# The final norm of an adaLN block moved into the block of the expert tiles

## The reference

```python
out = sum over the token's two experts of weight * (gelu(x @ w_up[e].T) @ w_down[e].T)
mu = mean(out); var = mean(square(out - mu))
out = (out - mu) * rsqrt(var + 1e-5)
ffn = out + x                      # x: the normalised, shifted input h
result = x_before + gb * ffn       # gb: one row of 128 per batch
```

## Time and profile before

| | |
|---|---|
| median of 3 runs | 1081.94 us (1081.14 to 1083.57) |
| the profiled execution | 1080.8 us, its span 1078.9 us |
| PE busy | 927.0 us, 86% of the span |
| VectorE, ScalarE, GpSimd busy | 847.5 (79%), 730.2 (68%), 557.8 us (52%) |
| tile block ends, closing block begins | 1042.3 us |
| closing block | 36.6 us to the span's end |

### The profile page before, as it was taken

One profiled execution on the slowest core, in us unless ns is written; L12 is line 12 of the kernel. 1 busy time (PEld: TensorE's weight loads), 2 busy tenths in 40 slices (PEclk: granted clock), 3 DMA queues, 4 the chain that ended last, 5 costly groups with the idle time before them and its releaser, 6 DMA issues. The chain is left out here.

```text
span 1078.9 us, 20269 instructions
## 1 busy us (share of the span) xinstructions
PE 927.0 (86%) x6154; PEld 666.3 (62%) x6154; DVE 847.5 (79%) x1731; ACT 730.2 (68%) x1927; POOL 557.8 (52%) x634
## 2 busy tenths in 40 slices
PE   4599999999999999999999999999996179999800
PEld 2366666666666667667666667666664167888600
DVE  5478888788878888888888888788876569988627
ACT  2278777778777777877777777777774256667504
POOL 1245446444665557465556646564673606766610
PEclk9999999999999999999999999999998579999955
DMA  7222322232222222222322232223122756676334
GB/s 241 53 50 50 74 50 50 50 73 61 50 64 72 60 64 69 60 53 73 79 50 50 64 85 57 56 74 77 45 60 97 237 195 244 244 238 236 126 104 130
DMA packets 67227, 104.27 MB, mean 97 GB/s; under 512 B 11115, under 2 KB 49912, under 8 KB 63536
## 3 DMA queue, kind: packets, MB, share of 16 engines
q1 hardware_dynamic: 59056, 90.53, 29.2%
q0 software_dynamic: 4992, 8.94, 2.8%
q10 hardware_dynamic: 3072, 3.51, 0.9%
HBM read 21.09 MB, written 15.50 MB: 34 GB/s over the span
## 5 line engine op out<-in xcount | busy, mean ns | idle before, releaser
L1173 POOL TENSOR_TENSOR four<-four 128x512 f32<-128x512 f32 x128 | 161.2, 1281 | 334.5 <-DVE ot L1119 213.8
L996 ACT ACTIVATE prob<-ps,nmax 128x512 f32<-128x512 f32 (+3 forms) x512 | 264.5, 529 | 76.1 <-DVE nmax L1096 76.1
L1096 DVE TENSOR_REDUCE nmax<-ps 128x2 f32<-128x1024 f32 (+3 forms) x256 | 211.0, 824 | 8.8
L915 PE MATMUL ps<-ident,prob 128*128 128x128 f32 x1280 | 191.4, 279 | 12.2 <-ACT probt L1017 6.9
L915 PEld LDWEIGHTS ps<-ident,prob 128*128 128x128 f32 x1280 | 142.2, 141 | 62.5 <-ACT prob L996 36.7
L1177 POOL TENSOR_TENSOR qk_lo<-four,qk_hi 128x512 fp32r<-128x512 f32 x128 | 162.3, 1291 | 0.0
L937 PE MATMUL ps<-probt,val 128*64 128x512 f32 (+3 forms) x1024 | 153.6, 442 | 0.2 <-ACT probt L1017 0.2
L1089 DVE TENSOR_TENSOR ps<-ps,tri 128x256 f32<-128x256 f32 x256 | 109.3, 427 | 53.5 <-PE ps L894 52.7
L1024 ACT CAST qk_hi<-four 128x512 fp32r<-128x512 f32 x128 | 79.5, 621 | 96.7 <-POOL four L1173 96.7
L1017 ACT COPY probt<-ps 128x512 f32<-128x512 f32 (+2 forms) x256 | 124.7, 520 | 19.6 <-PE ps L915 19.6
L1585 POOL DMA_INDIRECT results<-y,to_i x92 | 96.6, 1050 | 73.0 <-DVE y L1429 50.7
(11 more groups left out here) (222 smaller groups left out, 2163.4 us busy)
## 6 DMA issues: line engine op xcount, KB each, us to landing
four<-four SPq DMA_DIRECT2D x256, 128.0 KB
wt<-wall SPq DMA_DIRECT2D x23, 1024.0 KB, 4.8
xg<-slots SPq DMA_DIRECT2D x23, 288.0 KB, 3.8
hb<-h_hi SPq DMA_DIRECT2D x64, 64.0 KB, 2.1
hb<-h_lo SPq DMA_DIRECT2D x64, 64.0 KB, 2.0
y<-results SPq DMA_DIRECT2D x8, 512.0 KB, 7.3
x_all<-in_x SPq DMA_DIRECT2D x4, 512.0 KB, 10.6
h_hi<-rows SPq DMA_DIRECT2D x8, 256.0 KB, 2.7
```

The lines of the kernel that those rows point to most:

```text
L915: mm = e.transpose(ps[:, PT + at % 2, at_block * P:(at_block + 1) * P], prob[:, unit, kk * P:(kk + 1) * P], ident[:])
L996: e.activation(prob[:, unit, 0:w], ps[:, bank_s(idx) + j, 0:w], ACT.Exp, bias=nmax[:, q.par, idx, j:j + 1], accum_out=den[:, q.par, 2 * i ...
L1096: e.tensor_reduce(nmax[:, q.par, idx, :], ps[:, bank:bank + 2, 0:w], AX.X, ALU.max, negate=True).then_inc(v_max, 1)
L1173: e.tensor_tensor(qk[:, cols], tt[:, cols], ur[:, cols], op=ALU.add).then_inc(g_qk, 1)
```

## The change

The closing block is gone; its work stands behind the tile loop in the tile block, on the same engines, so one block end with its barrier falls away. SyncE waits for the landed scatters and for the weight copies and then issues the eight loads. The loaded rows `y2` and the products `z` (now one for each batch) lie in the SBUF of `wall`. ScalarE writes the normalised batch b into PSUM bank (b + 4) mod 8, and VectorE multiplies out of that bank. The factors of the second half come after the first product in place of after four products and adds. GpSimd does the adds of batches 0 to 3, VectorE those of 4 to 7; SyncE stores in order of batches, on two semaphores. The functions `end_sums`, `end_begin` and `end_factors` hold the former instructions of L1644 to L1661 unchanged.

```diff
+            plain = wall[:].rearrange("p x k i -> p (x k i)").bitcast(F32)
+            y2 = plain[:, 0:NT * 2 * E].rearrange("p (n k f) -> p n k f", k=2, f=E)
+            z = plain[:, NT * 2 * E:NT * 2 * E + B * S].rearrange("p (a t f) -> p a t f", a=B, f=E)
+            minus = sb(ph, "minus", [P, NT])
...
+            def norm_of(b):
+                return ps[:, (b + 4) % B, :].rearrange("p (t f) -> p t f", f=E)
...
+            def load_results(e):
+                for p in range(3):
+                    e.wait_ge(d_wt[p], 16 * ((NTL + 2 - p) // 3))
+                for p in range(4):
+                    e.wait_ge(d_ys[p], 16 * TB * ((NTL + 3 - p) // 4))
+                yv = ys.rearrange("(n p k) f -> p n (k f)", p=P, k=2)
+                for b in range(B):
+                    n = slice(b * TB, (b + 1) * TB)
+                    e.dma_start(y2[:, n].rearrange("p n k f -> p n (k f)"), yv[:, n, :]).then_inc(d_y2[b], 16)
...
+            def end_norm(e, g):
+                n = half_rows(g)
+                e.wait_ge(v_var, g + 1)
+                e.activation(tmp[:, 3, n], tmp[:, 1, n], ACT.Sqrt).then_inc(a_root, 1)
+                for b in range(g * PER, (g + 1) * PER):
+                    e.wait_ge(v_fac, g + 1)
+                    e.wait_ge(v_y, NTL)
+                    for t in range(TB):
+                        m = b * TB + t
+                        ins = e.activation(norm_of(b)[:, t, :], y2[:, m, 0, :], ACT.Identity,
+                                           bias=minus[:, m:m + 1], scale=rstd[:, m:m + 1])
+                    ins.then_inc(a_z, 1)
+            def end_gate(e, b):
+                e.wait_ge(a_z, b + 1)
+                e.tensor_tensor(z[:, b], norm_of(b), over(b), op=ALU.mult).then_inc(v_z, 1)
+            def end_result(e, b):
+                m = slice(b * TB, (b + 1) * TB)
+                e.wait_ge(v_z, b + 1)
+                e.wait_ge(v_g, 2 * B)
+                e.tensor_tensor(x_all[:, m, :], x_all[:, m, :], z[:, b], op=ALU.add).then_inc(v_out[b // PER], 1)
@@ tile block, SyncE, after the tile loop
+                    load_results(e)
+                    for b in range(B):
+                        n = slice(b * TB, (b + 1) * TB)
+                        e.wait_ge(v_out[b // PER], b % PER + 1)
+                        e.dma_start(ov[:, n, :], x_all[:, n, :]).then_inc(d_out, 16)
+                    e.wait_ge(d_out, 16 * B)
@@ ScalarE, after the tile loop
+                    for g in range(HALVES):
+                        end_norm(e, g)
@@ VectorE, after the tile loop
+                    for b in range(PER):
+                        end_sums(e, b)
+                    end_begin(e, tick, 0)
+                    end_factors(e, tick, 0)
+                    for b in range(PER, B):
+                        end_sums(e, b)
+                    end_begin(e, tick, 1)
+                    end_gate(e, 0)
+                    end_factors(e, tick, 1)
+                    for b in range(1, PER):
+                        end_gate(e, b)
+                    for b in range(PER, B):
+                        end_gate(e, b)
+                        end_result(e, b)
@@ GpSimd, after the tile loop
-                    for p in range(4):
-                        e.wait_ge(d_ys[p], 16 * TB * ((NTL + 3 - p) // 4))
-        with ExitStack() as ph:
-            y2 = sb(ph, "y2", [P, NT, 2, E])
...
+                    for b in range(PER):
+                        end_result(e, b)
```

More of the change, by code:

```diff
@@ L1266, in adaln_kernel @@
             tiles = sb(ph, "tiles", [P, 4, NTL])
+            plain = wall[:].rearrange("p x k i -> p (x k i)").bitcast(F32)
+            y2 = plain[:, 0:NT * 2 * E].rearrange("p (n k f) -> p n k f", k=2, f=E)
+            z = plain[:, NT * 2 * E:NT * 2 * E + B * S].rearrange("p (a t f) -> p a t f", a=B, f=E)
+            minus = sb(ph, "minus", [P, NT])
+            HALVES = 2
+            NH2 = NT // HALVES
+            PER = B // HALVES
+            d_y2 = [sem(f"e_y2{b}") for b in range(B)]
@@ new lines, in adaln_kernel, with half_rows @@
+            v_sum, v_st, v_dve, v_var, a_root, v_fac, a_z, v_z, v_out0, v_out1, d_out = (
+                sem("e_" + n) for n in ("sum", "st", "dve", "var", "root", "fac", "z", "vz", "out0", "out1", "dout"))
+            v_out = (v_out0, v_out1)
+            def norm_of(b):
+                return ps[:, (b + 4) % B, :].rearrange("p (t f) -> p t f", f=E)
+            def half_rows(g):
+                return slice(g * NH2, (g + 1) * NH2)
+            def load_results(e):
[7 more added lines that the diff above has]
+                    e.dma_start(y2[:, n].rearrange("p n k f -> p n (k f)"), yv[:, n, :]).then_inc(d_y2[b], 16)
@@ new lines, in end_sums, with end_begin @@
+            def end_sums(e, b):
+                m = slice(b * TB, (b + 1) * TB)
+                e.wait_ge(d_y2[b], 16)
+                e.tensor_tensor(y2[:, m, 0, :], y2[:, m, 0, :], y2[:, m, 1, :], op=ALU.add).then_inc(v_sum, 1)
+                e.wait_ge(v_sum, b + 1)
+                for t in range(TB):
+                    e.bn_stats(stats[:, b * TB + t, :], y2[:, b * TB + t, 0, :]).then_inc(v_st, 1)
+            def end_begin(e, tick, g):
+                n = half_rows(g)
+                e.wait_ge(v_st, NH2 * (g + 1))
+                factors_begin(v_dve, tick, e, lambda k: stats[:, n, k], mean[:, n],
+                              [tmp[:, i, n] for i in range(3)]).then_inc(v_var, 1)
@@ new lines, in end_factors @@
+            def end_factors(e, tick, g):
+                n = half_rows(g)
+                e.wait_ge(a_root, g + 1)
+                factors_end(v_dve, tick, e, rstd[:, n], tmp[:, 3, n], [tmp[:, i, n] for i in range(3)]).then_inc(v_dve, 1)
+                e.wait_ge(v_dve, tick.after(1))
+                e.scalar_tensor_tensor(out=minus[:, n], in0=mean[:, n], scalar=-1.0, in1=rstd[:, n],
+                                       op0=ALU.mult, op1=ALU.mult).then_inc(v_fac, 1)
+            def end_norm(e, g):
+                n = half_rows(g)
+                e.wait_ge(v_var, g + 1)
[3 more added lines that the diff above has]
+                    e.wait_ge(v_y, NTL)
+                    for t in range(TB):
+                        m = b * TB + t
+                        ins = e.activation(norm_of(b)[:, t, :], y2[:, m, 0, :], ACT.Identity,
+                                           bias=minus[:, m:m + 1], scale=rstd[:, m:m + 1])
+                    ins.then_inc(a_z, 1)
@@ L1483, in _ @@
                             copy_weights(e, j, col)
+                    load_results(e)
+                    ov = out.rearrange("(n p) f -> p n f", p=P)
+                    for b in range(B):
[3 more added lines that the diff above has]
+                    e.wait_ge(d_out, 16 * B)
                 @block.tensor
@@ L1575, in _ @@
                             dve_y(e, q // IC)
+                    tick = Count()
+                    for b in range(PER):
[12 more added lines that the diff above has]
+                        end_result(e, b)
                 @block.gpsimd
```

## The result

The changed kernel took 1071.67 us (median of 4 runs, 1069.55 to 1073.9), the kernel before in the same comparison 1082.76 us (4 runs, 1081.14 to 1084.12). The two medians lie 11.1 us apart. The ratio on record is 0.9914 with a 95% interval of 0.9895 to 0.9934, which is 7.1 to 11.4 us of the kernel before.

A forecast was written before the change was run, and what follows sets the result against it. After the last tile, VectorE's 23.1 us wait, with GpSimd's 8.882 us drain in it, was taken as the bound. Span 1078.9 to 1069.9 saves 9.0 us: 1071.8 from the profiled run, 1072.9 from the median; prediction 1072.4, range 1067.5 to 1075.5.

The forecast's parts named there:

- Boundary: Between tile loop and closing work: SyncE takes over the scatter waits, so the loads go out 9.3 us earlier.
- Rival C: At the old block end: the drain waited for the scatters' data, so no change, 1081.1 us; chance 0.03.
- D: In the tile loop: ScalarE table loads of 1.28 us placed at each of 23 tiles, 1101 us; chance 0.02.
- Price of the drain: GpSimd's drain, now at the program's end: 0.082 us per scatter since the last drain, 8.9 us for 108.
- A: At the closing drain: cost is time since the last scatter, so already settled, 1068.7 us; chance 0.14.
- E: At the closing drain: VectorE holds off its reads and stretches it by up to 3.3 us, 1075.1 us; chance 0.06.
- Hold-off: GpSimd's adds beside VectorE: whoever starts first holds off the other's two-SBUF-input instruction; second-half factors 1.15 us late.
- Rival B: GpSimd's adds beside VectorE: no contention, drain and barrier end at 1068.1, time 1070.0 us; chance 0.16.
- The end: Program end: GpSimd's drain from 1060.8 costs 8.9 us, the barrier 0.25, giving span 1069.9.
- the other branch: VectorE's adds and the stores at the end: VectorE done at 1064.1, plus 2.7 us, ending at 1066.8.

The follow-up runs named there:

- E4: The kernel before, its closing block and order untouched, without the GpSimd drain at the end of the tiles' block: 1086.63 us, ratio 0.9928.
- E1: The changed kernel with one more GpSimd drain, right behind its last scatter and ahead of its four adds: 1083.38 us, ratio 0.9881.
- E7: The changed kernel with a further GpSimd drain after tile 11 of 23: 1081.16 us in one run.
- E2: The changed kernel with the adds of batches 0 to 3 on VectorE instead of GpSimd: 1083.08 us, ratio 0.9883.
- E6: The changed kernel with an early GpSimd drain and GpSimd's first add held back until the second half's factors are ready: 1077.51 us, ratio 0.9888.
- E3: The changed kernel with only the block end removed: old order, all adds on VectorE, normalised rows in SBUF: 1088.99 us, ratio 0.9941.
- E10: The changed kernel with an early GpSimd drain and all four first-half products ahead of the second half's factors: 1073.26 us in one run.

## Why the prediction was right

Point by point, with the predicted distances from the first load's issue (1033.05 there, 1031.17 measured):

- *Boundary.* Predicted 9.3 us, measured 9.6 in the stretch from the last scatter to the first load (11.87 against 2.27). SyncE sees the last scatter land 2.3 us behind its start; GpSimd's drain and the barrier are what stood between. E4 shows the drain to be the cause and the barrier worth 0.7 us. Rival C is out. The first load landed in 4.0 us (3.9 predicted), and from there no table load delays anything: the changed kernel has five in all, as before, and Sqrt's stands at 1019.86, ahead of the loads (D is out). One small misreading: VectorE is not without a gap from 1046.25 on, it stands 0.28 us for the first root, in both kernels.
- *Price of the drain.* Predicted 8.9 us behind GpSimd's fourth add, measured 8.9. E1, E4 and E7 show that it goes by the number of scatters and not by time or place. A is out, and so is E, by which VectorE's work would have stretched it: VectorE worked for the first 3.2 us of the drain, and it took 8.9 all the same.
- *Hold-off.* Predicted for the squaring: a delay of 1.15 us; measured 1.01 (1.18 instead of 0.17). GpSimd's fourth add was predicted 27.75 us behind the first load, measured 27.35; VectorE's last add 31.05 and 30.55. Both came earlier, in part since the adds were stretched less than forecast: VectorE's by 0.6 and 0.35 us, GpSimd's last three by 0.3 together (4.17 against three of 1.28). E2 and E6 take the overlap away and the 1.2 us with it. Rival B is out.
- *The end.* Predicted span end 36.85 us behind the first load, measured 36.5. The predicted time, 1072.4, is 0.7 above the measured median, and some of this nearness is luck: in the profiled executions the forecast was 1071.8 against 1069.55, of which 0.6 us is an error of the stretch (9.0 forecast, 9.6 measured) and 1.6 lie ahead of the last scatter, where the forecast saw no change and no run explains one.

One step was wrong though its number was not. The prediction let the other branch end 2.7 us behind VectorE's last add, 33.75 us behind the first load, and gave batch 4's store 3 us of slack. In fact five stores were bunched behind GpSimd's fourth add, and SyncE saw the last of them land 6.0 us behind it, 33.3 us behind the first load; with the 0.4 us of the barrier that is 33.7. So nothing showed until E6 moved VectorE's add and the end stayed. A first sign was there: SyncE leaves 2.8 us behind VectorE's last add in the changed kernel, 2.3 in the kernel before. In the changed kernel the drain covers this as well.

And a gain was given back: the reordering brings the factors forward by 3.7 us net (6.6 to 2.9 us behind the first gate), of which 0.6 arrives at the end (E3). The rest waits for the drain that GpSimd's adds push back, and with the drain out of the way (E1) in part for the stores. With the drain early and the adds on GpSimd the order is worth 2.4 us (E10 against E1).

## What to carry to other kernels

Look at what an engine still owes at the end of its stream. GpSimd's drain at a block's end costs 0.083 us for every indirect DMA (of 128 rows here) since the last drain: give it a place where GpSimd idles, and before any late work that is moved there. Work handed to a second engine is worth what its last piece allows downstream: here the stores were queued in an order that made the slower engine's last batch hold back the faster one's. And when an edit advances a branch and the end stays, the branch was not the one that ended last, even if its number fitted.

## What the hardware showed that was not expected

- In E10 a `tensor_scalar` of 16 columns with one SBUF input (L146) was also held off, 1.18 us instead of 0.17, ending with a GpSimd add. The prediction had named instructions with two SBUF inputs only. The Trainium skill, "SBUF — State Buffer", section "Who interferes with whom", says that `tensor_scalar` can enter a mode that takes both ports and so contend with GpSimd, when its operands meet certain conditions. The row agrees with this; in which mode the instruction ran no row shows.
- The same program's time ahead of the last scatter differs by chip: it began at 1028.9 and at 1038.2 in two executions of the changed kernel, while the stretch behind it repeated to 0.1 us. What makes the difference was not tried.
